# Mixture-of-experts stage: the width branch is taken per pair of tiles instead of per eight

## What is computed

```
logits = xf @ router_w.T                      # 4096 tokens, 8 experts
topw, sel = top_k(sigmoid(logits), 2)         # two experts per token, weights normalised
h = square(relu(xf @ w1[e]))                  # w1[e] is 256 x 256 (experts 0-3) or 256 x 512 (4-7)
out = sum over the two experts of (h @ w2[e]) * weight
```

## Time and profile before

| | us |
|---|---|
| three runs | 779.54 median (778.46 to 780.48) |
| the profiled execution, device time | 778.08 |
| its span, first to last instruction | 776.3 |
| expert stage in that span, first `x_turn` to the end | 525.9 to 776.3 |
| granted TensorE clock, mean share of full speed | 0.927 |

### The profile page before, as it was taken

The page is one execution under the profiler, slowest core; times in us unless marked ns, Lnnn a source line. Parts: engine busy times, 40 slices in busy tenths (PEclk is TensorE's granted clock), DMA queues, the critical chain, the costliest instruction groups (busy, mean ns, idle before and its releaser), DMA issues. The chain is left out here.

```text
span 776.3 us, 16107 instructions
## 1 busy us (share of the span) xinstructions
PE 629.6 (81%) x4950; PEld 545.7 (70%) x4950; DVE 470.6 (61%) x1218; ACT 309.2 (40%) x666; POOL 336.5 (43%) x312
## 2 busy tenths in 40 slices
PE   0179487999999999999999997307998998978873
PEld 0179366787777878878788775206997887878873
DVE  0157476687879778797887873636453454545441
ACT  3123025334453443535335354005553544455442
POOL 6733223230824608155271735142353443455474
PEclk9779789999999999999999999656998999999897
DMA  7470686010111102111020101332353444466563
GB/s 231 132 198 1 136 246 209 2 55 2 56 55 50 62 1 75 34 54 55 21 88 0 54 28 55 108 110 69 63 92 54 79 70 71 78 100 103 86 112 49
DMA packets 38621, 61.07 MB, mean 79 GB/s; under 512 B 6282, under 2 KB 31890, under 8 KB 37906
## 3 DMA queue, kind: packets, MB, share of 16 engines
q1 hardware_dynamic: 23266, 36.80, 16.2%
q0 software_dynamic: 14976, 22.10, 15.3%
q10 hardware_dynamic: 288, 1.05, 0.4%
HBM read 30.54 MB, written 28.34 MB: 76 GB/s over the span
## 5 line engine op out<-in xcount | busy, mean ns | idle before, releaser
L1440 POOL DMA_INDIRECT out<-y,token_at x72 | 113.1, 1571 | 128.9 <-SPq L1420 128.0
L701 POOL DMA_INDIRECT queue_d<-row,slot x64 | 64.1, 1002 | 164.0 <-DVE slot L1013 146.9
L1519 DVE SCALAR_TENSOR_TENSOR act_w<-relu,queue_rows 128x512 f32<-128x512 f32 (+1 forms) x72 | 45.6, 633 | 118.0 <-ACT relu L1464 97.7
L1177 PE MATMUL bank<-xt_hi,w_first 128*128 128x512 f32 x256 | 94.1, 413 | 0.9 <-DVE second_half L891 0.9
L1177 PE MATMUL bank<-w_first,xt_hi 128*128 128x512 f32 x256 | 84.0, 410 | 2.5 <-DVE xt_lo L881 1.5
L693 POOL TENSOR_TENSOR second_half<-second_half,q_inv 128x512 f32<-128x512 f32 x64 | 64.9, 1041 | 42.4 <-DVE q_inv L900 42.3
L751 ACT ACTIVATE second_half<-second_half 128x512 f32<-128x512 f32 x64 | 40.3, 631 | 88.0 <-DVE second_half L891 87.8
L759 ACT ACTIVATE k_exps<-bank,k_negmax 128x512 f32<-128x512 f32 x64 | 44.2, 691 | 75.1 <-DVE k_negmax L907 74.9
L1561 PE MATMUL bank<-w_hi,a_hi 128*128 x224 | 70.4, 314 | 0.4 <-DVE a_lo L1525 0.3
L1464 ACT ACTIVATE relu<-bank 128x512 f32<-128x512 f32 (+1 forms) x72 | 36.2, 503 | 77.3 <-PE bank L1561 77.3
L1561 PE MATMUL bank<-w_lo,a_hi 128*128 x224 | 63.8, 285 | 0.0
(11 more groups left out here) (174 smaller groups left out, 1570.6 us busy)
## 6 DMA issues: line engine op xcount, KB each, us to landing
queue_rows<-queue_d SPq DMA_DIRECT2D x74, 129.0 KB, 2.1
store<-in_L_ffn_w SPq DMA_DIRECT2D x4, 1536.0 KB, 9.2
out<-res SPq DMA_DIRECT2D x8, 512.0 KB, 2.9
h_d<-store SPq DMA_DIRECT2D x7, 512.0 KB, 8.9
h_in<-h_d SPq DMA_DIRECT2D x7, 512.0 KB, 3.9
wqk<-in_L_attn_w_qkv SPq DMA_DIRECT2D x1, 2048.0 KB, 8.0
queue_d<-filler SPq DMA_DIRECT2D x1, 1290.0 KB, 11.5
out<-y,token_at POOLq DMA_INDIRECT x72, 4.0
```

The source lines that it names most:

```text
L701: pool.indirect_dma_start(out=queue_d, in_=row[:, t, c, :], in_offset=None, out_offset=bass.IndirectOffsetOnAxis(ap=slot[:, TT * c + t:TT ...
L1177: last = nc.tensor.matmul(o, a, c, start=(n == 1), stop=(n == 3 * len(pairs)))
L1440: pool.indirect_dma_start(out=out, in_=y[:, j % RING, :], in_offset=None, compute_op=ALU.add, out_offset=bass.IndirectOffsetOnAxis(ap=toke ...
L1519: nc.vector.scalar_tensor_tensor(out=act_w[:, u % 2, 0:width], in0=relu[:, u % 2, 0:width], scalar=rows[:, u, DIM:DIM + 1], in1=relu[:, u ...
```

## The change

The branch is now taken for each pair of tiles (36 times per engine instead of 9). A pair is run wide if the tile two places before its first one has a wide expert, because the pair's first step still runs the last parts of the tile two places back. The word is still loaded once per eight tiles.

```diff
+TURN = 2
...
         words = []
-        for turn in range(TILES // SLOTS):
-            words.append(engine.value_load(table.word_of[0:1, turn:turn + 1], min_val=0, max_val=EXPERTS ** SLOTS - 1))
-            with engine.If((words[turn] & (EXPERTS - 1)) < WIDE):
-                for u in range(SLOTS):
+        for first in range(0, TILES, TURN):
+            if first % SLOTS == 0:
+                words.append(engine.value_load(table.word_of[0:1, first // SLOTS:first // SLOTS + 1], min_val=0,
+                                               max_val=EXPERTS ** SLOTS - 1))
+            tiles = [(j // SLOTS, j % SLOTS) for j in range(first, first + TURN)]
+            oldest = max(first - AHEAD, 0)
+            with engine.If(((words[oldest // SLOTS] >> (3 * (oldest % SLOTS))) & (EXPERTS - 1)) < WIDE):
+                for turn, u in tiles:
                     step(words, turn, u, MAXW)
             with engine.Else():
-                for u in range(SLOTS):
+                for turn, u in tiles:
                     step(words, turn, u, NARROW_W)
         return words
```

## The result

| | before | after |
|---|---|---|
| median | 779.0 us (775.57 to 780.48, 4 runs) | 761.4 us (759.62 to 762.82, 4 runs) |
| profiled execution, device time | 778.08 us | 761.26 us |
| its span | 776.3 us | 759.5 us |
| granted TensorE clock | 0.927 | 0.949 |

The ratio is 0.9768, 95% interval 0.9739 to 0.9797: faster by 2.3%. The prediction was 765.6 us with a range of 760.5 to 772; the time lies in the range, 4.2 us under the point.

The account below looks back on a forecast made before the run. PE's beat, broken by long jumps at turn boundaries, was taken to bound the wide half, SP and POOL the narrow half. Parts A and B gave 13.9 us, C and D nothing: median 765.6 us, range 760.5 to 772.

Parts of the forecast that it names:

- Part A: Wide half's boundaries, tiles 8 to 35: shorter jumps never go beyond the next block, so 10.33 us are saved.
- price of a long branch: In R1: branches of 3.5 us or more have some 0.6 us covered, lose about 2.9; 14 boundaries cost 41 us.
- Part B: Tiles 36 to 39: the 4 us branch goes, SP's beat rules; tile 39's add at 673.19 instead of 687.09.
- the late fetch: Near tile 37: PE runs into a block soon after jumping into the one before; 0 to 1 us, 0 taken.
- Part C: Tiles 39 to 71: PE loses four stalls, 16.8 us, but SP and POOL still take 81.46 us; gain 0.
- Part D: Added heads and short jumps: about 0.4 us per PE boundary, hidden in the wide half; narrow pair 4.1 us.
- R1: Rival: every taken jump waits for a fetch, however short; 867 us, chance 0.03.
- R2: Rival: PE kept at its lower clock through the narrow half; 790.8 us, chance 0.03.
- R3: Rival: the narrow half follows PE, so tile 71 starts 37.5 us earlier; 742 us, chance 0.04.
- its milder form: Narrow half: SP's steps shrink from 2.14 to 2.00 us, 4.3 us in all, so 761.3; called likelier than R3.
- R4: Rival: wide-half short jumps not hidden, or late fetches at several pairs; 6.4 us of gain lost, 772 us, chance 0.12.

Follow-up runs that it names:

- the kernel with long jumps: The changed kernel with 36 more PE branches, one before each pair, each over 560 instructions that never run: 968.95 us, ratio 1.2462.
- the kernel without a branch: The changed kernel with widths fixed when the program is written, 38 wide then 34 narrow tiles, no branch: 757.81 us, ratio 0.9742.
- turns of eight: The changed kernel's new rule (tile two places ahead) with TURN = 8 instead of 2: 780.12 us, ratio 1.002 to the kernel before.
- the 20-instruction branches: The changed kernel with 36 more PE branches, one before each pair, each over 20 instructions that never run: 760.26 us, ratio 0.9786.
- the lighter PE: The changed kernel with two of three parts of the second product left out in narrow tiles: 760.3 us, ratio 0.9764.
- the words loaded early: The changed kernel with SP loading one register a tile (flag packed into row number) and all nine words loaded before the first pair: 756.70 us, ratio 0.9708.

## Why the prediction was right, and where it was off

**Part A** was right to a tenth: 10.33 us predicted, 10.40 found at the add of tile 35 (predicted 662.49, came 662.42). Its reason stands by the pair of kernels with long and short extra jumps, and by the fetches inside the long branches. One head is long all the same, before tile 38. The branch began at 659.55, the fetch that it waited for at 659.86; it took 1.22 us, and 1.4 us later, at 662.50, the branch ended. So even a jump over 135 instructions waits where its block has not been fetched yet; the kernel with long jumps shows such waits at 11 of its 17 narrow heads.

The prediction's price of a long branch, "about 2.9 us are lost at each", was too low, and its own rows say so: two long branches and one gap of 0.77 us lost 10.33 us from tile 8 to tile 35, so 4.8 us each. The kernel with long jumps lost 5.1 a boundary. The price stood in a rival, not in the sum.

**Part B** was off by 1.1 us: 3.57 us predicted, 2.48 found. The add of tile 39 came at 674.21 instead of 673.19. The term that was mis-sized is the late fetch, "cost 0 to 1 us, and 0 taken": the 2.95 us branch made y of tiles 36 and 37 late (ACT wrote them at 665.57 and 668.53, and at 662.83 and 664.66 in the kernel without a branch). Where no branch before tile 38 is long and 38 tiles are wide, tiles 36 to 39 take 9.8 to 10.5 us instead of 11.79.

**Part C is the step that failed**: "none of it reaches the end, because SP and POOL take the same 81.46 us". They took 77.42. 2.85 of these 4.04 us lie in the four changes of expert, 1.19 in the 28 ordinary steps. The prediction took the waits at changes (5.87, 6.10, 5.82) as fixed. The table shows that they aren't: the first three took 4.1 to 4.5 us in 26 of the 39 cases of the thirteen other kernels in it, up to 6.2 in the rest, whatever the kernel. The profiled execution of before had three of the longest. The DMA view of the add before a change shows the same, tile 44's add in the kernel before and in turns of eight (last number: us from issue to landing):

```profile
out<-y,token_at POOLq DMA_INDIRECT x1, 5.5
...
out<-y,token_at POOLq DMA_INDIRECT x1, 3.9
```

A long wait at a change can cover PE's next stall. With shorter ones the stall shows. In the run of turns of eight, whose branches are the same, POOL's timeline at tiles 53 and 54:

```profile
728.43 1.55 POOL L1445 DMA_INDIRECT out<-y,token_at  x1 [0.53 <-SPq L1425]
733.11 1.56 POOL L1445 DMA_INDIRECT out<-y,token_at  x1 [3.13 <-SPq L1425]
```

That ordinary step took 4.68 us, because y of tile 54 was late after a 4.46 us branch of PE (ACT wrote it at 731.52, 8.6 us after that of tile 53); in the profile of before the same step took 2.06. SP's own waits in this half say the same, between the adds of tiles 39 and 71, first in turns of eight, then in the kernel before:

```profile
SPq L118 <- DMA out<-y,token_at: 10.8, 8, 3.1
SPq L1419 <- ACT y L1481: 8.5, 10, 2.7
```

```profile
SPq L117 <- DMA out<-y,token_at: 14.4, 8, 3.9
SPq L1414 <- ACT y L1476: 3.3, 7, 0.8
```

In these two profiles one of the waits takes the place of the other, and the half takes 81 to 82 us either way. Without long stalls it takes 75.6 to 77.7 with the same SP; 75.60 is the kernel of the same 40 wide tiles without a branch. So PE's stalls and SP's beat were nearly level in the kernel before, and removing the stalls was worth 4 to 7 us there, not 0. What makes one landing take 4 and another 6 us was not found, nor is it shown that PE's stalls have no part in it.

**Part D** was right in that the added heads and short jumps hardly show: 0.07 to 0.42 us each on PE, 0.034 to 0.050 on ACT, 0.1 us lost from tile 8 to 35, and 1.2 us there with 36 more of them. Taken together with the one long branch they cost at most the 3.6 us by which the kernel without branches is faster.

Of the rivals, R1 (every jump waits) fell with the 20-instruction branches. R2 (the lower clock) did not occur with pairs, granted 0.99 in the narrow half; once every pair stalls it comes in part, 0.73 to 0.81. R3 in its strong form fell with the lighter PE; its milder form, shorter steps of SP, was not the cause either, 2.10 us instead of 2.14. R4 did not happen in the wide half. The sum by terms in the profiles: predicted 10.33 + 3.57 + 0 = 13.9, found 10.40 + 2.48 + 4.04 - 0.1 = 16.8 us; by the medians 17.6. That the time lies in the range is in part luck: its lower end was put there for SP's shorter steps (761.3 us), and these gave 28 x 0.04, some 1 us; the rest of what the sum lacked lies in the stalls and waits that part C had at nothing.

## What to carry to other kernels

Before a branch is shortened or removed, read the duration of the branch itself on the engine's sequencer, and count the instructions that it goes over in blocks of 256: here a jump that ended in the present or the next block, once that was there, cost PE's sequencer 0.2 to 0.4 us and one beyond 3 to 5, so a chain of short jumps beat a few long ones. Where two engines take nearly the same time, one profile can show one of them as the bound only because its waits happened to be long; compare the same waits in a second execution before a stall is costed at nothing. And a sequencer that only loads registers and issues DMAs can be the beat of a stage: one register load more on it cost each tile 0.48 us, and one less gained 0.14 us, or 0.23 with the words loaded early, before the next limit was met.

## What the runs showed of the hardware

- A jump's price on PE has steps, not a slope: 0.17 to 0.44 us over 20 to 371 instructions when it ends in a block that is there, 2.95 to 5.2 us when the fetch of its block began 0.3 to 2.2 us after the branch. A few lie between, 1.2 to 2.2 us, where the fetch had begun before the branch. Most branches of over 1 us ended 1.3 to 1.5 us after their fetch had ended. The same branches on ACT took 0.034 to 0.050 us. The Trainium skill ("Advanced Engine Details and Errata", section "Control Flow Timing") gives some 51 ns for an unconditional and 108 ns for a conditional branch; the trace names all branches here compare-and-branch, those that end a wide body too, ACT's took less than half of the second price, and PE's taken ones 1.6 to 4 times as long as it.
- After a jump out of the loaded blocks a second jump soon after can wait again: 11 of 17 narrow heads, 3.1 to 3.8 us, in the run with long jumps.
- The landing of an indirect add varies: a change of expert, which waits for it, took 3.8 to 6.2 us for the same work in the narrow half.
